# The second layer's mix: two products of 64 rows by 128 columns, or four of 64 by 64

## The chip, the cores and the metric

One core of one Trainium2 chip runs the whole kernel. The metric is the device time of one execution in microseconds (us); several executions are timed and their median is given.

## The reference, cut to what matters

The input is 16 images of 128 channels and 64 by 64 pixels. Each goes through two layers, each of which adds its result to the image. The first is a 3 by 3 convolution of the normalised and quantised image with three planes of weights. The second, which the change touches, is per pixel:

```
z = _gn(x)                                  # per image and group of 4 channels
q, k, v = Wq @ z, Wk @ z, Wv @ z            # 64 rows each
ek = exp(k)
num = exp(B) @ (ek * v);  den = exp(B) @ ek # 64x64 products
o = q * (num / den)                         # 64 rows
x = x + Wm @ o                              # Wm: 128x64, the "mix"
```

## The kernel before, in words

Five engines run instruction streams written out by hand, ordered by a common list of 36 slots (`SLOTS`) for each image and tied together by semaphores. In the phase of image p, TensorE (PE) runs the first layer of image p: `middle` and `outer` call `taps` (lines 476 to 478), nine fp16 products of 128 by 128 weights and 504 or 512 columns each, in runs. Between these runs stand the pieces of the second layer of the image before. An image has four pieces k (`NG`), each of 1024 pixels; each piece goes through `CYCLE` = 9 slots: `keys_values` (slot 1 of 9), `numerator_denominator` (3), `queries` (6) and `mix` (7), on PE. In between, ScalarE (ACT) takes exponentials and the logarithm, VectorE (DVE) forms the weighted values (`weighted_values`, L1078), the ratio (`ratio`, L1085 to L1090) and the product with q (`gate`, L1096). `gate` writes the tile `rec` and raises the semaphore `o_ready`; `mix` waits for it, multiplies `rec` by the fp32 weights `wmf` into two PSUM banks and raises `mix_ready`; ACT then copies the banks out (`evict`, L784), and a DMA adds them to the image. For the last image all four pieces are worked on at once, after the last taps (`LAST_ORDER`), and DVE adds the banks to the image itself (`second_residual`, L1104).

A piece's 1024 pixels are folded: pixels 0 to 511 of the 64 rows of o lie on partitions 0 to 63 of `rec`, the rest on partitions 64 to 127 (in another order of the pixels, which does not matter here). `wmf` holds the transposed Wm twice, on partitions 0 to 63 and 64 to 127, with 128 columns. So the mix of a piece is two products, one on each half of the rows of PE's array, each 64 rows deep, 128 columns wide, over 512 pixels. The first writes bank 0, the second bank 1.

`numerator_denominator`, called the sums below, already works on quadrants: eight fp32 products of 64 by 64 weights (`eb2`) over 256 pixels each, four of them at a time on the four quadrants of the array. Its wait goes through the helper `waits_apart`, which waits for `consts_made` (long since raised) and for the named semaphore as separate waits. The trace shows every fp32 product as two weight loads and two matmuls.

The waits that order PE against the others in the second layer are `o_ready` (DVE, for `mix`), `ratio_ready` (DVE, for `queries`) and `ekv_ready` (DVE, for the sums).

Of the kernel before, what the change touches and what calls it, by code (L numbers as in the profile page):

```python
# [29 lines left out]
IC = 64  # L30
# [3 lines left out]
NG = H // ROWS  # L34
# [58 lines left out]
def conv_layers_kernel(nc, x, g_pos, g_neg, bias, in_factor, out_factor, Wq, Wk, Wv, Bm, Wm, out):  # L93
# [6 lines left out]
    with ctx:  # L100
        def sb(name, shape, dt=F32):
            return ctx.enter_context(nc.sbuf_tensor(name, shape, dt))

        def sem(name):
            return ctx.enter_context(nc.semaphore(name))
# [37 lines left out]
        def work(name, dt, size):  # L143

            first = sb(name, [P, size], dt) if dt == F16 else second[("ek", "ekv", "rec").index(name)]
            half_words = size * (2 if dt == F32 else 1)
            out = [first[:, :] if dt == F16 else first]
            src, at = (last_f, free_f) if name == "rec" else (last_t, free_t)
            for k in range(1, NG):
                piece = src[:, at[0]:at[0] + half_words]  # L150
                out.append(piece.bitcast(F32) if dt == F32 else piece)
                at[0] += half_words
            return out
# [6 lines left out]
        rec = work("rec", F32, HALF)  # L160
# [21 lines left out]
        wmf = sb("wmf", [P, P])  # L182
# [26 lines left out]
        banks = [[t[:, 0, :], t[:, 1, :]] for t in (last_pair, A[0], A[1], low_pair)]  # L209
# [88 lines left out]
        o_ready = sem("o_ready")  # L298
# [5 lines left out]
        def waits_apart(eng, *waits):  # L304

            values = [v if isinstance(v, int) else eng.to_reg(v) for _, v in waits]
            eng.wait_ge(consts_made, 1)
            for (s, _), v in zip(waits, values):  # L310
                eng.wait_ge(s, v)
# [27 lines left out]
        def nth(image, per_image, m, back=0):  # L339

            return image * per_image + (m + 1 - back * per_image)
# [100 lines left out]
        def _(pe):  # L442
# [131 lines left out]

            def mix(image, k, w):

                pe.wait_ge(o_ready, nth(image, NG, k))
                for h in range(2):
                    half = slice(h * IC, (h + 1) * IC)
                    last = nc.tensor.matmul(banks[w][h], wmf[half, :], rec[w][half, :], start=True, stop=True)  # L580
                last.then_inc(mix_ready, 1)

            def second_layer(image, c):

                k, at = divmod(c, CYCLE)
                if at == L2_PE[0]:
                    keys_values(image, k, 0)
                if at == L2_PE[1]:
                    numerator_denominator(image, k, 0)
                if at == L2_PE[2]:  # L590
                    queries(image, k, 0)
                if at == L2_PE[3]:
                    mix(image, k, 0)

            def phase(p, m, images):
# [28 lines left out]
                if not cur:  # L624
                    for stage, k in LAST_ORDER:
                        if stage == "keys_values":
                            keys_values(p - 1, k, k)
                        elif stage == "sums":
                            numerator_denominator(p - 1, k, k)
                        elif stage == "queries":  # L630
                            queries(p - 1, k, k)
                        else:
                            mix(p - 1, k, k)
# [749 lines left out]
```

## Time and profile before

| | |
|---|---|
| median of 3 runs | 1584.97 us |
| the runs | 1585.08, 1582.66, 1584.97 us |
| the profiled execution, its own time | 1582.16 us |
| its span in the trace | 1580.4 us |
| mean granted clock of PE in it | 0.98 of 2.4 GHz |
| PE busy | 1456.5 us, 92% |
| DVE busy | 1390.4 us, 88% |
| ACT busy | 1162.4 us, 74% |

The span runs from the first to the last instruction; 1.8 us of the execution's own time lie around it. PE stands for the matmuls and PEld for the weight loads, which the trace keeps apart; L580 is line 580 of the kernel. A matmul's record is longer than the time for which it keeps the next one waiting, so that the start of the next record is what counts.

### The profile page before, as it was taken

What the parts mean: (1) busy time and instruction counts of PE and PEld (TensorE: products, weight loads), DVE (VectorE), ACT (ScalarE), POOL (GpSimd) and SP (SyncE); (2) the same over time, 40 slices, a digit from 0 to 9 for tenths busy, and PEclk for the clock granted to TensorE, in tenths of its full rate; (3) what the DMA queues carried; (4) which work ended last, traced back from release to release, by engine and by line L of the source; (5) the groups of instructions that cost most, each with busy time, mean ns of one, the idle gap of its engine ahead of it and who ended that gap; (6) DMA issues with size and microseconds to landing.
All of it is one profiled execution on the core that took longest, in us unless ns stands there. A gap on an engine that the chain in (4) does not pass through costs nothing.

```text
span 1580.4 us, 22708 instructions
## 1 busy us (share of the span) xinstructions
PE 1456.5 (92%) x7792; PEld 622.2 (39%) x7792; DVE 1390.4 (88%) x2165; ACT 1162.4 (74%) x1511; POOL 503.9 (32%) x505
## 2 busy tenths in 40 slices
PE   1499999999999999999999999999999999999864
PEld 1254434344443434444344433434443443444322
DVE  3879899998989899998989998898999989898646
ACT  4357778786877878787778878787777878776444
POOL 2221324242433333333333333333342423424212
PEclk9699999999999999999999999999999999999987
DMA  5010111313222231323113132311313132111231
GB/s 201 1 54 15 40 28 40 108 41 107 54 60 75 55 107 28 107 54 91 49 49 107 28 107 56 98 49 41 107 28 111 50 107 54 41 41 41 67 80 54
DMA packets 29173, 103.80 MB, mean 66 GB/s; under 512 B 4032, under 2 KB 4224, under 8 KB 29056
## 3 DMA queue, kind: packets, MB, share of 16 engines
q1 hardware_dynamic: 20416, 70.86, 12.2%
q0 software_dynamic: 8640, 31.46, 10.5%
q8 instruction: 64, 1.05, 0.3%
q14 instruction: 53, 0.43, 0.1%
HBM read 37.29 MB, written 33.55 MB: 45 GB/s over the span
## 4 chain that ended last, share of the span: by engine, by line
PE 74%; DVE 18%; issue 4%; ACT 2%; POOL 1%; DMA 0%; DVEq 0%; SPq 0%; POOLq 0%; ACTq 0%
PE A L476 13%; PE A L478 12%; PE A L477 12%; PE L L536 7%; PE B L476 7%; PE B L478 7%; PE B L477 7%; PE L L580 4%; PE L L567 3%; DVE uall L1069 1%; DVE duo L987 1%; ACT junk L707 1%; DVE A L1039 1%; DVE duo L1036 1%; DVE uall L1042 1%
## 5 line engine op out<-in xcount | busy, mean ns | idle before, releaser
L476 PE MATMUL A<-T,WH 128*128 128x504 f16 (+1 forms) x1152 | 439.8, 382 | 1.0 <-ACT uall L731 1.0
L477 PE MATMUL A<-T,WH 128*128 128x504 f16 (+1 forms) x1152 | 438.2, 380 | 0.0
L478 PE MATMUL A<-T,WL 128*128 128x504 f16 (+1 forms) x1152 | 438.0, 380 | 0.0
L1308 POOL TENSOR_TENSOR T<-t,T 128x512 f16<-128x512 f32 x192 | 245.6, 1304 | 412.5 <-ACT T L689 412.5
L707 ACT ACTIVATE junk<-xr,shift 128x1024 f16<-128x1024 f32 x256 | 293.9, 1148 | 12.4 <-DVE xr L1072 5.2
L1282 POOL TENSOR_TENSOR zl<-z,zh 128x512 f16<-128x512 f32 x120 | 150.9, 1277 | 398.8 <-ACT zh L764 397.8
L476 PE MATMUL B<-T,WH 128*128 128x504 f16 (+1 forms) x576 | 221.2, 384 | 29.6 <-POOL T L1308 20.5
L478 PE MATMUL B<-T,WL 128*128 128x504 f16 (+1 forms) x576 | 220.3, 382 | 0.9 <-issue 0.9
L477 PE MATMUL B<-T,WH 128*128 128x504 f16 (+1 forms) x576 | 220.5, 383 | 0.0
L476 PEld LDWEIGHTS A<-T,WH 128*128 128x128 f16 x1152 | 115.3, 100 | 196.1 <-issue 83.8
L478 PEld LDWEIGHTS A<-T,WL 128*128 128x128 f16 x1152 | 112.9, 98 | 136.9 <-issue 1.1
L477 PEld LDWEIGHTS A<-T,WH 128*128 128x128 f16 x1152 | 112.9, 98 | 111.6 <-issue 0.8
L689 ACT CAST T<-t 128x512 f16<-128x512 f32 x192 | 105.7, 614 | 51.9 <-DVE t L1003 51.9
L536 PE MATMUL L<-zh,wqkv 128*64 128x512 f16 x732 | 103.8, 392 | 33.9 <-DVE shared L1090 30.3
L731 ACT CAST uall<-A 128x1024 int16<-128x1024 f32 x96 | 96.3, 1003 | 44.1 <-PE A L478 41.9
L1315 POOL DMA_DIRECT2D xr<-shared x60 | 54.2, 903 | 172.1 <-ACT shared L784 171.9
L476 PEld LDWEIGHTS B<-T,WH 128*128 128x128 f16 x576 | 56.6, 98 | 127.6 <-issue 61.4
L764 ACT CAST zh<-z 128x1024 f16<-128x1024 f32 x60 | 62.7, 1045 | 54.8 <-PE L L536 53.4
L723 ACT COPY m<-B 128x1024 f32<-128x1024 f32 x96 | 95.5, 994 | 7.5 <-PE B L478 7.5
L774 ACT ACTIVATE shared<-L 128x512 f32<-128x512 f32 x61 | 36.3, 595 | 78.2 <-PE L L567 78.2
L964 DVE SCALAR_TENSOR_TENSOR f<-f,q 128x1024 f32<-128x1024 f32 x64 | 90.2, 1410 | 1.9 <-ACT f L679 1.9
L1036 DVE TENSOR_TENSOR duo<-A,m 128x512 f32<-128x512 f32 x96 | 66.1, 688 | 26.6 <-PE A L478 21.9
(153 smaller groups left out, 2449.0 us busy)
## 6 DMA issues: line engine op xcount, KB each, us to landing
xr<-in_x_dram SPq DMA_DIRECT2D x64, 512.0 KB, 5.8
out_dram<-xr SPq DMA_DIRECT2D x64, 512.0 KB, 2.7
xr<-shared POOLq DMA_DIRECT2D x60, 512.0 KB, 4.6
xr<-in_L_conv_g_pos_dram SPq DMA_DIRECT2D x3, 576.0 KB, 9.9
xr<-in_L_conv_g_neg_dram SPq DMA_DIRECT2D x3, 576.0 KB, 11.2
xr<-in_L_conv_Wm_dram SPq DMA_DIRECT2D x2, 32.0 KB, 10.4
xr<-in_L_conv_Wq_dram SPq DMA_DIRECT2D x1, 32.0 KB, 11.2
xr<-in_L_conv_Wk_dram SPq DMA_DIRECT2D x1, 32.0 KB, 10.9
```

The lines of the kernel that those rows point to most:

```text
L476: nc.tensor.matmul(to, wh, th, start=fresh and y == 1, stop=False, skip_group_check=True)
L477: nc.tensor.matmul(to, wh, tl, start=False, stop=False, skip_group_check=True)
L478: done = nc.tensor.matmul(to, wl, th, start=False, stop=y == 2, skip_group_check=True)
L536: last = nc.tensor.matmul(out, lhsT, src, start=m == 0, stop=m == 2, skip_group_check=True)
L689: nc.scalar.copy(T[:, 0, pair, g * TILES:(g + 1) * TILES, :, :], t32[:, pair]).then_inc(th_ready, 1)
L707: nc.scalar.activation(junk[:, :], src[:, q * PX:(q + 1) * PX], func, bias=shift[which][:, :], accum_out=moments[which][:, k, q:q + 1]).th ...
L723: nc.scalar.copy(m2[:, :, :], low_pair[:, :, :]).then_inc(m2_copied, 1)
L731: nc.scalar.copy(u[i].rearrange("p (t k c) -> p k t c", k=4, c=W)[:, 0:4:3], A[n % 2][:, :, :].rearrange("p e (t w) -> p e t w", w=W)).the ...
L964: nc.vector.scalar_tensor_tensor(out=f_rows(q), in0=f_rows(q), scalar=KAPPA, in1=integers(q), op0=ALU.add, op1=ALU.mult).then_inc(f_ready, 1)
L1036: nc.vector.tensor_tensor(minus, near, m2[:, 0, :], ALU.subtract)
L1282: nc.gpsimd.tensor_tensor(zl[0][:, cols], z32[:, cols], zh[0][:, cols], ALU.subtract).then_inc(zl_ready, 1)
L1308: last = nc.gpsimd.tensor_tensor(low, t32[:, pair, :, :, :].rearrange("p t e w -> p (t e w)"), high, ALU.subtract)
```

## The change

`mix` computes the same from the same tiles into the same places. Each of its two products is split by columns into two of 64 by 64, so that there are four, one on each quadrant of the array, and the wait for `o_ready` goes through `waits_apart`.

```diff
             def mix(image, k, w):
 
-                pe.wait_ge(o_ready, nth(image, NG, k))
-                for h in range(2):
-                    half = slice(h * IC, (h + 1) * IC)
-                    last = nc.tensor.matmul(banks[w][h], wmf[half, :], rec[w][half, :], start=True, stop=True)
+                waits_apart(pe, (o_ready, nth(image, NG, k)))
+
+                for r in range(2):
+                    rows = slice(r * IC, (r + 1) * IC)
+                    for c in range(2):
+                        cols = slice(c * IC, (c + 1) * IC)
+                        last = nc.tensor.matmul(banks[w][r][cols, :], wmf[rows, cols], rec[w][rows, :],
+                                                start=True, stop=True)
                 last.then_inc(mix_ready, 1)
```

## Rows read from the trace of the kernel before

**Rows 1.** The page: busy times, and the chain that ended last by engine

```profile
PE 1456.5 (92%) x7792; PEld 622.2 (39%) x7792; DVE 1390.4 (88%) x2165; ACT 1162.4 (74%) x1511; POOL 503.9 (32%) x505
...
PE 74%; DVE 18%; issue 4%; ACT 2%; POOL 1%; DMA 0%; DVEq 0%; SPq 0%; POOLq 0%; ACTq 0%
```

**Rows 2.** The chain in order of time, one image: start, length, what

```profile
1214.45 0.70 DVE shared L1090
1215.20 0.84 PE L L536 x6
...
1218.09 1.06 PE L L580 x4
...
1230.50 1.02 PE L L567 x16
...
1240.29 1.06 PE L L580 x4
...
1262.62 1.06 PE L L580 x4
...
1284.95 1.06 PE L L580 x4
...
1288.16 0.69 DVE duo L1036
...
1308.83 1.06 PE L L580 x4
```

**Rows 3.** DVE's timeline at that handover: start, length, instruction, idle before

```profile
1288.16 0.69 DVE L1036 TENSOR_TENSOR duo<-A,m 128x512 f32<-128x512 f32 x1 [0.59 <-PE A L478]
```

**Rows 4.** PE's timeline around one mix, first pair and second pair apart

```profile
1217.71 0.38 PE L478 MATMUL A<-T,WL 128*128 128x504 f16 x1
1218.02 0.70 PE L580 MATMUL L<-shared,wmf 64*128 64x512 f32 x2
...
1218.55 0.59 PE L580 MATMUL L<-shared,wmf 64*128 64x512 f32 x2
...
1219.08 0.39 PE L476 MATMUL B<-T,WH 128*128 128x512 f16 x1
```

**Rows 5.** PE's timeline in one block of sums: rounds 1, 2 and 4

```profile
1206.24 0.38 PE L478 MATMUL B<-T,WL 128*128 128x504 f16 x1
1206.55 0.45 PE L567 MATMUL L<-shared,eb 64*64 64x256 f32 x4
...
1206.82 0.40 PE L567 MATMUL L<-shared,eb 64*64 64x256 f32 x4
...
1207.25 0.40 PE L567 MATMUL L<-shared,eb 64*64 64x256 f32 x4
```

**Rows 6.** By source line, weight loads: duration in ns, least, median, most

```profile
L580 PEld LDWEIGHTS L<-shared,wmf x244: 182/186/330, 215.1 to 1568.9; 64*128 64x128 f32 x122
...
L567 PEld LDWEIGHTS L<-shared,eb x976: 129/133/133, 203.7 to 1557.9; 64*64 64x64 f32 x196
```

**Rows 7.** PE's timeline: start of the products of the queries

```profile
1215.20 0.41 PE L536 MATMUL L<-zh,wqkv 128*64 128x512 f16 x2 [1.61 <-DVE shared L1090]
```

**Rows 8.** DVE's timeline: the gate before the mix of rows 4

```profile
1216.19 0.68 DVE L1096 SCALAR_TENSOR_TENSOR shared<-L,shared 128x512 f32<-128x512 f32 x1
```

**Rows 9.** Timeline where PE waited for a gate, and for weighted values

```profile
1481.61 0.69 DVE L1096 SCALAR_TENSOR_TENSOR shared<-L,shared 128x512 f32<-128x512 f32 x1 [1.30 <-PE L L536]
...
1482.35 0.70 PE L580 MATMUL L<-shared,wmf 64*128 64x512 f32 x2 [0.79 <-DVE shared L1096]
...
1520.49 0.69 DVE L1078 SCALAR_TENSOR_TENSOR shared<-L,shared 128x512 f32<-128x512 f32 x1
...
1521.33 0.61 PE L567 MATMUL L<-shared,eb 64*64 64x256 f32 x5 [1.51 <-DVE shared L1078]
...
1528.25 2.08 PE L580 MATMUL L<-shared,wmf 64*128 64x512 f32 x4 [0.79 <-DVE shared L1096]
```

**Rows 10.** PE's waits: total, times, longest; 200 to 1471 us, then the span

```profile
PE L L536 <- DVE shared L1090: 23.2, 14, 2.0
...
PE L L580 <- DVE shared L1096: 2.4, 3, 0.8
```

**Rows 11.** Busy times of 757 to 761 us; PE's clock after POOL's column

```profile
757.00:761.00 4.00, 3.90 (x13) 1.30 (x14) 3.70 (x7) 3.33 (x6) 1.31 (x2) 0.57 0.02 6
```

**Rows 12.** The chain across that stretch, and the same step in a later image

```profile
735.76 1.06 PE L L580 x4
...
761.63 1.06 PE L L580 x4
...
1194.21 1.06 PE L L580 x4
```

**Rows 13.** The chain's last pieces

```profile
1571.51 0.69 DVE f L1096
1572.20 2.39 DVE xr L1104 x4
1574.59 0.60 DVEq L100
1575.19 1.79 DVE xr L1104 x3
```

## The prediction, made before the changed kernel ran

> **What bounds the kernel now.** I read the page first, for busy times and for the chain that ended last. PE is busy for 92% of the span, DVE for 88%, and the chain lies on PE for 74% and on DVE for 18% [rows 1]. With two engines that full, the question is where in an image each one leads, so the next view is the chain in order of time over one image [rows 2]. The pattern repeats every 90.74 us (1218.09 to 1308.83). From 1215.20, when the queries start, to 1288.16 the chain is on PE; from there to the next queries it is a sequence of DVE instructions that ends in L1090. All four mixes of the image stand on the PE part, with 1.06 us each. DVE sat idle for 0.59 us before it took the chain over [rows 3]. So PE can become some 0.6 us faster per image before DVE would have led that point anyway.
>
> That tells what a shorter mix is worth: all that it saves, four times an image. Then comes what a mix costs PE, from the timelines around one mix and around one block of sums, which already uses quadrants [rows 4, 5].
>
> **What the two products cost.** A matmul holds back the next by less than its record's length, so I go by starts. The last tap before the mix starts at 1217.71, the mix at 1218.02 (0.31 later), the second pair of records at 1218.55 and the next tap at 1219.08 [rows 4]. "x2" at one start says that both 64-row halves of the array work side by side. A pair therefore takes 0.53 us, and the whole mix 1.06.
>
> **What four quadrants would cost.** The sums run four records at once, over 256 columns, in four rounds: starts at 1206.55, 1206.82, (1207.04) and 1207.25 [rows 5]. Rounds two and three take (1207.25 - 1206.82) / 2 = 0.215 us each; the first takes 0.27. A round over 512 columns then takes 0.43, and a mix on quadrants has two such rounds: each of its four products has two records, and four products run at a time. Its streaming is 2 x 0.43 = 0.86, as much as the four rounds of the sums, 4 x 0.215 = 0.86. The two products of before also have two rounds: the streaming does not get shorter. All 128 columns of a half were used before, and a quadrant's product goes over as many pixels.
>
> What differs is the rest. The mix's block is 1.06 - 0.86 = 0.20 us of rest, the block of sums is 1.02 on the chain [rows 2], so 1.02 - 0.86 = 0.16. The source of it is visible: the first round is longer than a later one by 0.53 - 0.43 = 0.10 us in the mix, and by 0.27 - 0.215 = 0.055 in the sums. This is the first weight load, which nothing covers: 128 columns take a record of 186 ns, 64 columns 133 ns, 0.053 less [rows 6]. The later loads run under matmuls in both. The four quadrants give about 0.01 back, since their starts are staggered and the last ends later. So a mix goes from 1.06 to 1.02: **0.04 us less**. Entering is unchanged, 0.31 us from the last tap's start for either form (1206.24 to 1206.55, and 1217.71 to 1218.02) [rows 4, 5]. Four more loads and matmuls per mix are in this figure, since the sums issue twice as many and still fill their rounds.
>
> The bounds: with the starts rounded to 0.01, the saving is 0.03 at least; with the full 0.053 of the load and no stagger it is 0.053 at most.
>
> **The wait.** With `waits_apart` the wait for `o_ready` becomes an instruction of PE's queue, behind which its loads, matmuls and the following taps are queued. What does it cost when the gate ended early? The gate before this mix ran from 1216.19 to 1216.87, 1.15 us before the mix started [rows 8], and the mixes of the 14 images look alike. The same kind of wait stands before the sums, whose blocks start 0.31 after their tap all the same [rows 5]. So nothing in the steady state. Where PE does wait for DVE, the price shows: from the end of the gate to the mix took 1482.35 - 1482.30 = 0.05 with the old wait, from the end of the weighted values to the sums 1521.33 - 1521.18 = 0.15 with the other [rows 9]. So **0.10 us more** where the gate is late. PE waits so for the gate three times [rows 10], all in the image before the last, where its other work is thinner, and once at half clock, where the mix takes 2.08 and would save 0.08 [rows 9]. The three come to 2 x 0.06 + 0.02 = +0.14.
>
> **The last image.** Its four mixes stand at the very end. The chain is DVE there: the last gate, then eight additions of L1104 one after another to the end [rows 13]. The mixes are done before DVE asks for their banks; shortening them brings nothing. In that tail I put 0.
>
> **The sum.** 56 mixes in steady state x 0.04 = -2.24 us, the fourth one of the image before the last -0.04, its three late ones +0.14: **-2.1 us**. By the bounds, 56 x 0.03 - 0.14 = 1.5 and 56 x 0.053 = 3.0. On the profiled execution, 1582.16 becomes 1580.0 and its span 1580.4 becomes 1578.3. The three runs and this one spread from 1582.16 to 1585.08, so that the profiled one is a quick example. From the median, 1584.97, the sum gives 1582.8; from the mean of all four, 1583.7, it gives 1581.6. I take a value between, 1582.2.
>
> **A rule that speaks against this order.** The queries start two products at once, at the same 1215.20, on the same 128 rows of the array and on neighbouring column halves [rows 7]. So column neighbours with the same rows run together in this trace, in fp16. The changed mix issues its quadrants in just that order, both column halves of rows 0 to 63 and then both of rows 64 to 127, while the sums alternate the rows. The Trainium skill, page "TensorE: Matmul & The Clock Gate", section "Part 3: Packing small matmuls — row/col tiling", says that a weight load overlaps matmuls in flight only when its row group differs. By that rule the second column half would have to wait for the first. The rows of the queries disagree, but for fp16 and full rows.
>
> **The rivals.**
>
> *Serialised column halves.* If in this order the fp32 products of the same rows do not overlap, each mix gets the second quadrant's two rounds on top: 2 x 0.43 = 0.86, less 0.04, is +0.82. With 60 mixes on the chain that is +49 us, 1633. For it speaks only that no row shows fp32 quadrants in this order; against it the queries, and the sums, whose third product shares its rows with the first and still starts in the same round ("x4") [rows 5, 7]. Chance 0.04.
>
> *The separate wait is late.* The place is the mix in steady state, where the gate must end more than about 0.15 us before the mix's turn. There it ends 1.15 us before [rows 8]. If something pushed it past that point, each mix would lose 0.10 - 0.04 = 0.06, over 60 mixes +3.6 us: 1588. Chance 0.04.
>
> *The saving is hidden.* If DVE set the pace in the PE part too, nothing would move: 1584.4. DVE's idle 0.59 against 0.16 saved per image speaks against it [rows 3]. Chance 0.06.
>
> *The clock.* In each of the 14 images of the steady state PE waits up to 2.0 us for L1090 [rows 10]. After one such wait the granted clock fell: 0.57 on average from 757 to 761, between the levels 2.4 and 1.2 GHz [rows 11]. The step from the fourth mix to the next image's first then took 761.63 - 735.76 = 25.87 us, against 1218.09 - 1194.21 = 23.88 in a later image [rows 2, 12]. So an episode costs 2.0 us, as much as the whole gain. The change shifts each of these waits by another 0.16 us, and may meet one episode more (1584.2) or one fewer (1580.2). The wait itself stays equally long, so I give each 0.13.
>
> The plain sum has 0.58, and 0.02 is left for what I do not see.
>
> **How the numbers follow.** About 0.2% (3.2 us) is what a measurement of this kernel can tell from no change. The sum, 2.1, lies inside, and with the spread of the runs it may be read on either side: of its 0.58, 0.20 go to faster and 0.38 to same. One episode fewer is mostly faster (0.11 of 0.13), one more mostly same (0.12). The hidden saving is same (0.06), the late wait half slower and half same, serialised halves slower. With the rest shared out: faster 0.33, same 0.60, slower 0.07. The range takes in the bounds of the sum (1.5 to 3.0) and one episode either way, from 1579.8 to 1585.3; it leaves out the serialised and the late cases.
>
> **What the profile after should show.** L580 with eight matmuls and eight loads per mix, of 64x64 weights, loads of about 133 ns; four records in one round, about 0.48 to the second round and 1.02 from the mix's start to the next tap. On PE one more separate wait per mix, over 1 us ahead of it. An image's period of 90.74 - 0.16 = 90.58 us. The prediction is wrong if records of one mix stand in four rounds, if the last tap and the mix are more than 0.31 apart in steady state, or if the period does not shrink though the block does.

## The result, and the profile after

| | before | after |
|---|---|---|
| median | 1584.6 us (18 runs, 1582.42 to 1589.62) | 1582.29 us (18 runs, 1577.68 to 1586.10) |
| ratio after to before | | 0.9983, 95% interval 0.9975 to 0.9992 |
| profiled execution, own time | 1582.16 us | 1582.16 us |
| its span | 1580.4 us | 1580.4 us |

The changed kernel is 2.3 us faster by the medians, and the interval leaves out "no change", if narrowly. The two profiled executions took the same time to 0.01 us. That is chance, and the trace shows what it is made of.

The page of the changed kernel has 576 instructions more, 9 for each of the 64 mixes (four loads, four matmuls, one wait), with PE's busy time as before and 5 us less weight loading. These are its counterparts to [rows 1]:

```profile
span 1580.4 us, 23284 instructions
...
PE 1456.1 (92%) x8048; PEld 617.1 (39%) x8048; DVE 1391.2 (88%) x2165; ACT 1162.5 (74%) x1511; POOL 504.0 (32%) x505
```

The chain in order of time, over the image that [rows 2] shows (`mix` is now L583, L1090 is now L1094, L1036 now L1040):

```profile
1213.21 0.70 DVE shared L1094
...
1213.95 0.84 PE L L536 x6
...
1216.85 1.02 PE L L583 x8
...
1229.22 1.02 PE L L567 x16
...
1239.00 1.02 PE L L583 x8
...
1261.30 1.02 PE L L583 x8
...
1283.59 1.02 PE L L583 x8
...
1286.75 0.69 DVE duo L1040
...
1307.42 1.02 PE L L583 x8
```

A mix takes 1.02 on the chain instead of 1.06, just what the sums take, and the image's period is 1307.42 - 1216.85 = 90.57 us instead of 90.74.

PE's timeline around this mix, in three narrow stretches as in [rows 4]: all four quadrants, the second round alone, the next tap.

```profile
1216.46 0.38 PE L478 MATMUL A<-T,WL 128*128 128x504 f16 x1
1216.77 0.66 PE L583 MATMUL L<-shared,wmf 64*64 64x512 f32 x4
...
1217.25 0.61 PE L583 MATMUL L<-shared,wmf 64*64 64x512 f32 x4
1217.80 0.39 PE L476 MATMUL B<-T,WH 128*128 128x512 f16 x1
```

"x4" at one start: the four quadrants run side by side. The entry is 0.31 as before, the second round follows after 0.48 instead of 0.53, and the next tap 1.03 after the mix's start instead of 1.06 (1.02 where the loads are counted; the starts are rounded). The loads by source line, the answer to [rows 6]: 132 ns instead of 186.

```profile
L583 PEld LDWEIGHTS L<-shared,wmf x488: 129/132/228, 217.0 to 1568.8; 64*64 64x64 f32 x163
```

**Why the two profiled spans agree.** The times of the first mix, of the 56th (the last of the steady state) and of the end split a span into three parts. They come from the starts of the mixes in each trace; in the table stand also the runs below that repeat one of the two kernels or change its mix slightly.

| run | first mix at | 1st to 56th mix | 56th mix to end | mix 24 to 25 | mix 33 to 37 |
|---|---|---|---|---|---|
| before | 215.13 | 1251.09 | 114.18 | 25.87 | 93.15 |
| before, again | 216.22 | 1251.20 | 114.26 | 25.86 | 93.35 |
| after | 216.97 | 1247.57 | 115.86 | 24.19 | 93.30 |
| after, again | 216.71 | 1246.66 | 115.40 | 24.18 | 92.41 |
| after, old wait outside the loop | 216.41 | 1247.54 | 115.65 | 24.19 | 93.27 |
| after, rows alternating | 215.55 | 1249.00 | 117.26 | 25.62 | 93.09 |
| after, eight tiles | 216.90 | 1247.36 | 114.54 | 24.19 | 93.07 |

In the profiled pair, the start took 1.84 us longer. All of it lies ahead of the first mix, and the same kernel before gave 215.13 and 216.22. The middle is 3.52 shorter: 55 mixes x 0.04 = 2.20, 1.64 more because the fall of the clock of [rows 11] is absent (25.87 - 0.04 - 24.19), and 0.31 given back where PE branches to the loop's head (93.30 - (93.15 - 0.16)). The end is 1.68 longer, the starts counted from a mix's first load: 0.10 for the late gates, and 1.59 in the stretch from the 60th to the 61st mix (42.07 instead of 40.49), where the clock stayed low for longer. The windows of that stretch show it, PE's clock third from the right, before and then after:

```profile
1545.00:1560.00 15.00, 8.21 (x58) 3.47 (x62) 8.27 (x15) 7.88 (x11) 9.26 (x10) 0.63 0.01 2
```

```profile
757.00:761.00 4.00, 3.01 (x19) 1.25 (x23) 3.93 (x7) 3.83 (x6) 0.89 (x1) 1.00 0.01 2
...
1545.00:1560.00 15.00, 9.54 (x58) 3.78 (x62) 7.93 (x13) 6.98 (x9) 10.39 (x11) 0.55 0.00 0
```

The first row of the second fence answers to [rows 11]: at 757 to 761 us PE now kept its full clock. In the last image the chain goes through the first queries and sums, and there the price of the low clock can be read off, first before, then after: 0.62 and 1.07 us grow to 1.06 and 1.96.

```profile
1556.85 0.62 PE A L536 x4
1557.47 1.07 PE L L567 x16
```

```profile
1555.52 1.06 PE A L536 x4
1556.59 1.96 PE L L567 x16
```

### The profile page after: what moved, and what is told of

Same layout as the page of the kernel before. It is cut to its first block, busy times and chain, and to the rows that moved or that the text cites. A ratio compares the mean times of both kernels' runs of the same rounds, so it can differ in the third digit from the quotient of the medians.

```text
span 1580.4 us, 23284 instructions
## 1 busy us (share of the span) xinstructions
PE 1456.1 (92%) x8048; PEld 617.1 (39%) x8048; DVE 1391.2 (88%) x2165; ACT 1162.5 (74%) x1511; POOL 504.0 (32%) x505
## 4 chain that ended last, share of the span: by engine, by line
PE 72%; DVE 20%; issue 5%; ACT 2%; POOL 1%; DMA 0%; DVEq 0%; SPq 0%; POOLq 0%; ACTq 0%
PE A L476 13%; PE A L478 12%; PE A L477 12%; PE L L536 7%; PE B L476 7%; PE B L478 6%; PE B L477 6%; PE L L583 4%; PE L L567 3%; DVE uall L1073 1%; DVE duo L991 1%; ACT junk L711 1%; DVE A L1043 1%; DVE duo L1040 1%; DVE uall L1046 1%
## 5 line engine op out<-in xcount | busy, mean ns | idle before, releaser
L1040 DVE TENSOR_TENSOR duo<-A,m 128x512 f32<-128x512 f32 x96 | 66.1, 688 | 25.1 <-PE A L478 20.4
```

Of the source, the lines that this page charges most:

```text
L1040: nc.vector.tensor_tensor(minus, near, m2[:, 0, :], ALU.subtract)
```

## The experiments

Lines of a changed kernel shift by a few against those of before; `mix` and its operands tell them apart. A ratio is that to the kernel before, from runs of the same session.

**1. Both kernels once more.** The changed kernel again, and the kernel before again, unedited, to tell what belongs to a kernel from what belongs to an execution.

> The changed kernel once more, to have a second profile of it. The theory (the first weight load theory) is that a mix saves 0.040 us because half of its uncovered first weight load is gone, and that 56 of 60 such savings arrive at the end: 1.0 us-sized differences of single executions are then from the start and the end of the run, where PE's clock is low. Expected: a mix's block 1.019 us from its first load to the next tap's, gate to mix 0.115 us in the three late ones, image period 90.58 us, ratio 0.998 to 0.999. A rival, that the steps of 1 to 2 us at the start and end belong to the change, would show the first mix again 1.8 us later than in the kernel before, and the last stage again 1.6 us longer.

> The kernel before once more, for a second profile. If the step near 960 us, where PE's queue branches back to the head of the loop over the images, is a matter of where the code lies (placement theory), PE stops there as in the first profile: about 1.5 us after the branch and 1.3 us a little later. If it is chance, the gaps differ. The first mix may start anywhere within 2 us of 215.1, and a fall of the clock near 757 may be there or not: these are chance.

Measured: the changed kernel 1581.45 us (11 runs), ratio 0.9989 (0.9978 to 1.0000). Its profile has the same 1.02 us per mix and a period of 90.57, the first mix at 216.71, and 40.68 from the 60th to the 61st mix, so the 42.07 of the first profile is not in every execution of this kernel. Its end was nevertheless 1.2 us longer than that of the kernel before (115.40 against 114.18), now from the 56th to the 60th mix (63.05 instead of 62.03), where the granted clock was low for about twice as long. The kernel before (a single run, 1583.73 us) had its first mix at 216.22 and its two stops near 960 us as in the first profile (1.11 and 1.15 us of idle time, against 1.15 and 0.91 there). So the step at the start comes and goes with one kernel. That of the last two images changed its place; whether it belongs to the change, this pair of profiles does not tell.

**2. The separate wait alone.**

```diff
-                pe.wait_ge(o_ready, nth(image, NG, k))
+                waits_apart(pe, (o_ready, nth(image, NG, k)))
                 for h in range(2):
                     half = slice(h * IC, (h + 1) * IC)
                     last = nc.tensor.matmul(banks[w][h], wmf[half, :], rec[w][half, :], start=True, stop=True)
```

> The kernel before with the separate wait alone, its two products kept. First weight load theory: the block stays at 1.059 us, entry 0.31, no saving; only the three mixes whose gate is late start 0.06 us later (0.115 instead of 0.052 after the gate), and the ratio is 1.000, at most 1.0003. Rival, that the separate wait brings the saving (loads issued earlier): block 1.02 us, ratio 0.9985. Rival, that the separate wait costs in the steady state: the taps or the mix start later than 0.31 after the last tap, period above 90.74.

Measured: 1586.66 us, ratio 1.0014 (1.0004 to 1.0023). The mix keeps its 1.06 us and the period its 90.74, so the wait brings none of the saving and costs nothing in the steady state. The three late mixes start 0.06 later and take 0.03 longer. But the kernel was slower, which I had not expected: of the 3.4 us by which its middle part is longer, all lie at one place, from the 33rd to the 37th mix (96.58 instead of 93.15). PE's timeline, with idle time before an instruction in brackets:

```profile
959.16 0.38 PE L478 MATMUL A<-T,WL 128*128 128x504 f16 x1
963.75 0.60 PE L476 MATMUL B<-T,WH 128*128 128x512 f16 x1 [4.21 <-issue]
```

This is just behind the branch of PE's queue to the head of the loop over images. PE idles for 4.21 us and the tap after it runs at half clock (0.60 instead of 0.39). The kernel before has two shorter stops there:

```profile
958.21 0.38 PE L478 MATMUL A<-T,WL 128*128 128x504 f16 x1
959.74 0.39 PE L476 MATMUL B<-T,WH 128*128 128x512 f16 x1 [1.15 <-issue]
...
962.55 0.39 PE L478 MATMUL B<-T,WL 128*128 128x504 f16 x1 [0.91 <-issue]
```

and the changed one has only the first of them:

```profile
958.58 0.39 PE L476 MATMUL B<-T,WH 128*128 128x512 f16 x1 [1.10 <-issue]
```

**3. Is it where the code lies?** Three runs: the separate wait alone once more; the kernel before with idle waits at the start of PE's queue, which only move its later code; and the separate wait with more of them, to bring the loop's head to about where the changed kernel has it.

> The separate wait alone, once more. In its first run PE stood still for 4.6 us after the branch back to the loop's head (1.2 us of it after the branch, 3.1 more before the first tap), against 1.5 and 1.3 in the kernel before, and the ratio was 1.0014. Placement theory: the gap of 4.6 us is there again and the ratio is 1.001 to 1.002. Rival, chance: a gap of 1.2 to 2 us, ratio 1.000.

> The kernel before with 17 idle waits at the very start of PE's queue (on a semaphore already raised), as many instructions as the separate waits of the mixes put ahead of the loop's head. Nothing else changes, so the loop's code only lies 17 instructions further on. Placement theory: the long stop near 960 us appears, gap above 3 us, ratio 1.001 to 1.002. Rival, that the stop belongs to the separate waits in the loop: gaps as in the kernel before (1.5 and 1.3), ratio 1.000.

> The separate wait alone, and 136 idle waits at the start of PE's queue, so that the loop's head lies where the changed kernel has it (17 mixes ahead of the loop, eight more loads and matmuls each). PE is idle at the start for other reasons, which covers the 7 us that they take. Placement theory: the long stop near 960 us is gone, gap about 1.5 us as in the changed kernel, ratio 0.999 to 1.000. Rival, that the stop belongs to the separate waits: gap of 4.6 us, ratio 1.0014.

The edit, with 17 and 136 for n:

```diff
-            pe.wait_ge(consts_made, 1)
+            for _ in range(1 + n):
+                pe.wait_ge(consts_made, 1)
             group_stats(0, 0)
```

Measured, in the order of the runs: the repeat 1587.24 us, ratio 1.0021 (1.0009 to 1.0034); the kernel before with idle waits 1586.12, ratio 1.0008 (0.9996 to 1.0021); the longer shift 1584.71, ratio 0.9998 (0.9983 to 1.0013). The pages show 8 and 68 added instructions instead of 17 and 136, so two waits went into one and the loop moved by half of what I had meant. In the third run it lies 17 + 68 = 85 instructions further on than in the kernel before, where the changed kernel has it 17 x 9 = 153 further on. The stops at the branch in the three:

```profile
963.60 0.60 PE L476 MATMUL B<-T,WH 128*128 128x512 f16 x1 [3.94 <-issue]
```

```profile
960.60 0.39 PE L476 MATMUL B<-T,WH 128*128 128x512 f16 x1 [1.09 <-issue]
...
963.62 0.61 PE L477 MATMUL B<-T,WH 128*128 128x504 f16 x1 [1.98 <-issue]
```

```profile
963.01 0.39 PE L476 MATMUL B<-T,WH 128*128 128x512 f16 x1 [0.93 <-issue]
```

The repeat has the long stop again, so it belongs to the kernel. With 8 idle waits ahead, the kernel before keeps its first stop, but its second comes four taps earlier and takes 1.98 instead of 0.91. With the separate waits in place and 68 instructions ahead, the second stop is gone. The distances fit: in the kernel before, the second stop stands ahead of the ninth tap after the branch. A tap is two instructions, a load and a matmul; 8 instructions further on it stands four taps earlier, ahead of the fifth, and with one wait for each of the 17 mixes that come before the loop's head eight taps earlier, ahead of the first. So the second stop follows from where the loop's code lies and not from the waits in it. The prediction of "above 3 us" for the second run missed: the shift was half, and the stop was shorter. In that run the middle part was 2.44 us longer than before. The third run did not gain from the missing stop: from the 33rd to the 37th mix it took 93.24. It had its first mix at 218.67, 2.6 later than the first run with the separate wait (216.10), so the waits added there may not have been free.

Fetching of instructions is the likely reason. While PE stood still in the run of experiment 2, from 960.6 to 963.6 us, the DMA queues carried packets of one kind alone:

```profile
q14 instruction: 2, 0.02, 2.4%
q8 instruction: 1, 0.02, 2.3%
```

In all five profiles with a second stop, the tap behind it starts 1.25 to 1.55 us after the end of such a packet of 16 KB on q8 (961.30 and 962.55 in the kernel before, 962.20 and 963.75 in experiment 2). The changed kernel has that packet too (958.95 to 959.94) and does not stop. That PE waits for what they bring is argued from these times, not shown.

In the changed kernel PE has one stop less here, and yet in the first profile the stretch from the 33rd to the 37th mix is no shorter (93.30), and in the repeat only by 0.6 more than the mixes save (92.41). Its chain there goes over DVE, which has a stop of its own at its branch (L366); the kernel before has it as well, 1.80 us of idle time:

```profile
957.14 0.69 DVE A L1052
957.83 1.89 issue
959.72 0.07 DVEq L366
...
959.84 0.71 DVE L L1089
```

**4. The old wait outside the loop.** In the images whose number is a constant, the wait goes with the first load again.

```diff
-                waits_apart(pe, (o_ready, nth(image, NG, k)))
+                if isinstance(image, int):
+                    pe.wait_ge(o_ready, nth(image, NG, k))
+                else:
+                    waits_apart(pe, (o_ready, nth(image, NG, k)))
```

> The changed kernel, but with the old kind of wait in all images outside the loop (the wait rides on the first weight load there), the separate one only inside the loop. First weight load theory: steady blocks stay at 1.019 us with either wait, and in the three late mixes the start after the gate goes from 0.115 back to 0.052 us and the block from 1.048 to 1.02, so 0.2 to 0.3 us are gained over the changed kernel in all: ratio about 0.9982, not to be told from the changed kernel by its times. Rival, that the quadrants need the separate wait to run together: blocks of over 1.1 us in the images outside the loop.

Measured: 1581.80 us (11 runs), ratio 0.9987 (0.9974 to 0.9999), against 1581.45 and 0.9989 of the changed kernel in the same session: not told apart, as expected. The mechanism can be read in the first late mix. The changed kernel first, then this one; the gate (L1100 and L1103) and the mix's first load:

```profile
1479.91 0.69 DVE L1100 SCALAR_TENSOR_TENSOR shared<-L,shared 128x512 f32<-128x512 f32 x1 [1.30 <-PE L L536]
...
1480.71 0.24 PEld L583 LDWEIGHTS L<-shared,wmf 64*64 64x64 f32 x8 [1.33 <-issue]
```

```profile
1479.31 0.69 DVE L1103 SCALAR_TENSOR_TENSOR shared<-L,shared 128x512 f32<-128x512 f32 x1 [1.30 <-PE L L536]
...
1480.05 0.21 PEld L586 LDWEIGHTS L<-shared,wmf 64*64 64x64 f32 x8 [1.27 <-DVE shared L1103]
```

From the gate's end to the load it is 0.11 us with the separate wait and 0.05 with the old one; the load's own time to the next tap is 1.05 and 1.02. So a late separate wait costs 0.09 us, and quadrants run together with either. From the 56th mix to the 60th the two differ by 0.30 us, as expected.

**5. Rows alternating.** The four products in the order of the sums.

```diff
-                for r in range(2):
-                    rows = slice(r * IC, (r + 1) * IC)
-                    for c in range(2):
-                        cols = slice(c * IC, (c + 1) * IC)
+                for c in range(2):
+                    cols = slice(c * IC, (c + 1) * IC)
+                    for r in range(2):
+                        rows = slice(r * IC, (r + 1) * IC)
```

> The changed kernel with its four products in the other order, as the sums have it: for each column half first rows 0 to 63, then rows 64 to 127. First weight load theory: order has no effect, the four start together, block 1.019 us, ratio 0.998 to 0.999. Rival, that neighbours on the same rows hinder each other (their loads or their reads of the same pixels): block shorter than in the changed kernel, by the part that is lost there, at most the 0.02 us of stagger.

Measured: 1584.65 us (10 runs, 1577.16 to 1586.21), ratio 1.0004 (0.9990 to 1.0017). The mix takes 1.02 us and the period is 90.58, so the order has no effect on the block, and column neighbours of the same rows hinder nobody. The ratio is higher than expected, with the same saving in the trace. Its profile has the fall of the clock at 757 to 761 us (0.61, and 25.62 us from the 24th to the 25th mix) and the long low clock before the 61st mix, and the mean granted clock of its ten runs is 0.979, against 0.981 for the kernel before in that session. That the clock hid the change in the total fits this, but is not shown apart from the order.

**6. Eight tiles.**

```diff
-                    for c in range(2):
-                        cols = slice(c * IC, (c + 1) * IC)
+                    for c in range(4):
+                        cols = slice(c * 32, (c + 1) * 32)
```

> Each product split by columns into four of 32 instead of two of 64: eight tiles of 64x32, same output, separate wait. First weight load theory with stagger: the first load shrinks again by half, 0.053 to 0.027 us, but eight products start 0.0067 us apart, so the last one starts 0.047 instead of 0.020 after the first: block 1.02 us as with four, ratio 0.998. Rival, that only the load counts: block 0.992 us and ratio 0.997. Rival, that eight do not fit side by side: four rounds, block about 1.88 us, ratio 1.03.

Measured: 1582.64 us, ratio 0.9995 (0.9986 to 1.0004), higher than the expected 0.998, though the period is 90.59. PE's timeline around a mix, sixteen records in the two rounds, the second round alone, the next tap; then the mix's loads by source line:

```profile
1216.49 1.09 PE L582 MATMUL L<-shared,wmf 64*32 64x512 f32 x16
...
1216.94 0.64 PE L582 MATMUL L<-shared,wmf 64*32 64x512 f32 x8
...
1217.51 0.39 PE L476 MATMUL B<-T,WH 128*128 128x512 f16 x1
```

```profile
L582 PEld LDWEIGHTS L<-shared,wmf x16: 102/104/106, 1216.5 to 1216.6; 64*32 64x32 f32 x16
```

1.02 us, as with four. Halving the first load once more would have brought 0.027; the stagger of eight products eats it. Eight tiles do run side by side. This run also shows the two parts of the saving one by one, which its total alone would not. With two, four and eight products the first load takes 183, 129 and 103 ns, and the second round starts 0.534, 0.480 and 0.453 us after the mix: it follows the load to within 1 ns. The last product of that round starts at 0.540, 0.500 and 0.500, and the next tap comes 0.522 after it in all three.

**7. Each mix twice.** The products of before, and the quadrants, computed twice over.

```diff
+                for again in range(2):
                     (the two products, or the four)
```

> The two products of 64x128 are computed twice in each mix, same result, separate wait; it adds work only. Streaming theory: both forms stream for the same time, 0.427 us a round, so the block goes from 1.059 to 1.059 + 0.857 = 1.92 us, and with 60 mixes on the chain the time rises by 51 us, to about 1636. Rival, that a mix on the chain is partly hidden: a rise well below 48 us.

> The four products of 64x64 are computed twice in each mix, same result, separate wait. Streaming theory: the same two extra rounds, 0.857 us, block 1.019 + 0.857 = 1.88 us, about 2.3 us below the run with the two products doubled, because the weight loads of the repeat are covered and the first one is saved once. Rival, that quadrants stream slower or faster than halves: the block grows by something else than 0.857, and the difference between the two doubled runs is not 0.04 us a mix.

The two products keep the old wait in this run, other than its expectation says; experiment 2 showed that the wait makes no difference to a block in the steady state.

Measured: 1636.41 and 1632.60 us (2 runs each), ratios 1.0337 (1.0317 to 1.0358) and 1.0313 (1.0293 to 1.0334). The chain has, for the two products and for the four:

```profile
1255.90 1.92 PE L L581 x8
...
1278.96 1.92 PE L L581 x8
```

```profile
1253.09 1.88 PE L L583 x16
...
1276.10 1.88 PE L L583 x16
```

Both forms grow by 0.86, so quadrants stream exactly as long as halves, and the difference stays 0.04, once per mix. The periods are 94.18 and 94.02, that is 3.44 more in both, 4 x 0.86: every mix's time arrives.

**8. Half of the pixels.** What would a much shorter mix bring? The kernel leaves out half of the mix's output.

```diff
-                        last = nc.tensor.matmul(banks[w][r][cols, :], wmf[rows, cols], rec[w][rows, :],
+                        last = nc.tensor.matmul(banks[w][r][cols, 0:QUART], wmf[rows, cols], rec[w][rows, 0:QUART],
```

> The changed kernel's mix leaves out half of its pixels: each of the four products goes over 256 instead of 512 pixels, so part of the output is not computed. It asks how much of a larger saving would still arrive. The block must fall from 1.019 to about 0.59 us, 0.47 below the kernel before. Theory A, that DVE's idle time of 0.59 us before it takes over is the limit per image: the period falls by at most 0.59, to 90.15, and the time by some 8.5 us, to 1576. Theory B, that DVE's idle time renews itself because the mixes also bring forward what DVE waits for, so only the fourth mix's own saving (0.47) is measured against 0.59: the period falls by 4 x 0.47 = 1.88, to 88.86, and the time by 26 us, to about 1558.

Measured: 1563.39 us (4 runs), ratio 0.9879 (0.9863 to 0.9896), 20 us less. The mix takes 0.59 and the period is 89.26, 1.48 below before: more than theory A's 0.59, less than theory B's 1.88. The chain shows what neither had, PE's wait for DVE before L521, the product for the statistics of the next image:

```profile
1240.08 0.98 DVE gin L946
...
1241.10 0.39 PE B L521 x2
...
1246.27 0.59 PE L L582 x8
...
1268.13 0.59 PE L L582 x8
...
1270.87 0.69 DVE duo L1039
```

Of the two mixes ahead of L521 only some 0.54 of 0.93 us arrives; of the two behind it, all 0.93 do, although the idle time of [rows 3] is 0.59.

## Why the prediction was right

**The size.** Predicted was 1582.2 us, from a sum of 2.1; measured are 1582.29 and a difference of 2.3. The sum's main term holds: 0.040 us per mix in the steady blocks, 2.20 over 55 of them. The streaming stayed at two rounds of 0.43 (experiment 7). The saving is the uncovered first load, 0.054 shorter, less 0.013 of stagger (experiment 6), and it arrives in full.

**The total agrees partly by luck.** The sum holds no term for the clock, and the profiled pair has two steps of 1.6 us of it, one each way, besides 1.8 us at the start. The rival "one episode fewer" came true in the middle of the span, and a longer low clock before the last image took it back. A fall of the clock between 757 and 764 us stood in all six profiles with a mix of 1.06 us (both of before, both with the separate wait alone, both with idle waits) and in one of the five with 1.02 us in the table. The time at which PE idles there may decide it, but eleven profiles are few: whether the change avoids this fall, or these executions happened to, stays open. It is worth 1.6 us, nearly as much as the saving itself.

The other profiles make chance less likely. The two products doubled (experiment 7) have a fall between the same two mixes, so it stands in seven of seven with two products; the quadrants doubled and those over half of the pixels (experiment 8, whose clock fell near 1109 us instead) do not, so it stands in one of seven with quadrants. The end leans the other way: from the 56th mix on, the six profiles with 1.06 us took 112.25 to 114.57, the five with 1.02 took 114.54 to 117.26. So the change seems to move the places where the clock falls, about as much for the worse at the end as for the better in the middle; that the two nearly cancel is luck for a sum without a term for the clock. Why the clock falls where it does stays open.

The prediction put an episode at 2.0 us, from a step of 25.87 against 23.88 in a later image. That was too much: this step takes 24.19 in the changed kernel, where the clock did not fall, so that 0.35 of it is not the clock, and 1.64 is.

The five ratios of kernels with the same saving, from 0.9983 to 1.0004, show how much of such a total is not the change.

**The wait.** 0.06 us was expected as the net price of a late gate, and 0.05 was measured. In the steady state it costs nothing by itself, in experiment 2 too. What the prediction had no term for is that an added instruction moves the code behind it. With the wait alone that cost 3.4 us at the loop's branch; in the changed kernel, with 8 instructions more per mix, it happened to remove a stop, and DVE's own stop hid most of that.

**Column neighbours on the same rows.** The rows of the queries pointed to no effect, and that is so for fp32 quadrants: "x4" at one start, and the same block in either order (experiment 5). By the Trainium skill, page "TensorE: Matmul & The Clock Gate", section "Part 3: Packing small matmuls — row/col tiling", a load overlaps running matmuls only where its row group differs; here the trace disagrees. The four loads for the second round start 0.05 to 0.07 us after the mix and take 133 ns each, while the second round starts only at 0.48: they run under matmuls on the same rows. That section of the Trainium skill also puts the issue of a further tile at about 4 ns; the trace has 7 ns here, the 0.02 us by which the fourth product trails the first, and 3 ns between the two fp16 products of the queries.

**How much more would arrive.** The prediction said that PE could become 0.6 us faster per image before DVE led the handover. That was too low: 1.48 of 1.87 arrived (experiment 8), since a shorter mix also brings forward what DVE waits for: at the handover all 0.47 arrived, and PE's wait for DVE behind it stayed at 1.61 us as before. And the first limit is another wait, that for L521. For 0.16 per image it made no difference.

## What to carry to other kernels

Splitting a product into more tiles of the array did not shorten its streaming here, where the array's width was full before; what it saved was a part of the one weight load that no matmul covers, and halving that once more was eaten by the stagger of the starts. The cheapest way to price a form that is not in the trace is another block of the same kernel that has it. When a change is worth 0.1 to 0.2%, compare the place itself in the two traces and split the rest of the span into parts, since a fall of the clock or a stop at a branch moves the total by as much.

## What the hardware showed that was not expected

- A few instructions more ahead of a loop change what the branch to its head costs. PE idled there for 1.15 + 0.91 us in the kernel before, 1.09 + 1.98 with 8 instructions ahead, 4.21 with a wait added per mix (3.94 in its repeat), 0.93 with 68 more ahead of that.
- After the stop of 4.21 us PE's taps ran at half clock at first, records of 0.60 instead of 0.39 us.
- Eight tiles of 64 by 32 run side by side in fp32, sixteen records in 1.02 us, as four of 64 by 64 do.
- A separate wait that is late costs 0.09 us more than one that goes with the load: 0.11 instead of 0.05 to the first load, and 0.03 more until the next tap.
